# One kernel: adapter sums of the first network by single sequences, their rows spread through DRAM

## The reference

```
def lora_add(base, inp, A, B):
    Ab = A[layer_idx][lora_indices]      # per sequence: 16 x 512
    Bb = B[layer_idx][lora_indices]      # per sequence: 1376 x 16
    t = einsum('bri,bni->bnr', Ab, inp)
    return base + einsum('bor,bnr->bno', Bb, t) * SCALE     # SCALE = 0.5
gate = lora_add(einsum('bnh,fh->bnf', x, W_gate), x, A_gate, B_gate)
up   = lora_add(einsum('bnh,fh->bnf', x, W_up), x, A_up, B_up)
act  = silu(gate) * up
x    = x + ffn(lora_add(einsum('bnf,hf->bnh', act, W_down), act, A_down, B_down))
```

## Time and profile before

| | |
|---|---|
| median of 3 runs | 606.76 us (606.46 to 607.78) |
| the profiled execution | 606.15 us, span 604.5 us |
| PE busy in the span | 99% |
| DVE, ACT, POOL busy | 78%, 49%, 48% |

### The profile page before, as it was taken

The page is one execution under the profiler, slowest core; times in us unless marked ns, Lnnn a source line. Parts: engine busy times, 40 slices in busy tenths (PEclk is TensorE's granted clock), DMA queues, the critical chain, the costliest instruction groups (busy, mean ns, idle before and its releaser), DMA issues.

```text
span 604.5 us, 8075 instructions
## 1 busy us (share of the span) xinstructions
PE 599.7 (99%) x2904; PEld 491.9 (81%) x2904; DVE 469.7 (78%) x572; ACT 295.3 (49%) x413; POOL 292.7 (48%) x219
## 2 busy tenths in 40 slices
PE   8999999999999999999999999999999999999997
PEld 7787887878778888888888878888788888888886
DVE  6797757757778999873459877645879998999987
ACT  5865224323443445441124445334658886478860
POOL 6135334324434055831034586520005889958897
PEclk9999999999999999999999999999999999999999
DMA  8896472541171215212121200342232221322203
GB/s 255 220 227 180 148 170 65 131 130 28 53 207 37 71 35 166 69 31 66 35 71 35 70 30 31 84 83 84 61 101 78 77 69 36 109 67 75 75 7 139
DMA packets 30475, 56.06 MB, mean 93 GB/s; under 512 B 10468, under 2 KB 14532, under 8 KB 30052
## 3 DMA queue, kind: packets, MB, share of 16 engines
q1 hardware_dynamic: 28932, 53.05, 30.7%
q0 software_dynamic: 1216, 1.98, 1.5%
q10 hardware_dynamic: 288, 0.52, 0.2%
HBM read 48.44 MB, written 6.06 MB: 90 GB/s over the span
## 4 chain that ended last, share of the span: by engine, by line
PE 99%; DVE 0%; issue 0%
PE ps_down L2355 7%; PE ps_down L2356 7%; PE ps_down L2357 7%; PE ps_gate L2458 3%; PE ps_gate L2639 3%; PE ps_gate L2638 3%; PE ps_up L2638 3%; PE ps_gate L2459 3%; PE ps_gate L2460 3%; PE ps_up L2639 3%; PE ps_m L2638 3%; PE ps_down L2638 3%; PE ps_m L2639 3%; PE ps_down L2639 3%; PE ps_up L2458 3%; PE ps_up L2459 2%
## 5 line engine op out<-in xcount | busy, mean ns | idle before, releaser
L1144 POOL TENSOR_TENSOR up_sum<-up_sum,up_more 128x1024 f32<-128x1024 f32 x14 | 33.7, 2409 | 62.6 <-DVE up_more L1926 62.6
L2355 PE MATMUL ps_down<-act_hi,w_hi 128*128 128x512 f32 x112 | 43.9, 392 | 0.0
L2356 PE MATMUL ps_down<-act_lo,w_hi 128*128 128x512 f32 x112 | 43.6, 390 | 0.0
L2357 PE MATMUL ps_down<-act_hi,w_lo 128*128 128x512 f32 x112 | 43.6, 389 | 0.0
L1026 POOL TENSOR_TENSOR cond_total<-w_raw 128x512 f32<-128x512 f32 x8 | 10.5, 1310 | 60.4 <-DMA w_raw<-in_cond_gu 36.3
L1691 DVE TENSOR_TENSOR w_lo<-w_total,w_hi 128x512 fp32r<-128x512 f32 (+1 forms) x28 | 28.8, 1030 | 13.3 <-ACT w_hi L1462 12.6
L1926 DVE SCALAR_TENSOR_TENSOR gate_sum<-ps_up,s_group,gate_sum 128x1024 f32<-128x1024 f32 x28 | 35.8, 1279 | 3.8 <-PE ps_up L2639 3.7
L1102 POOL TENSOR_TENSOR act_lo<-up,act_hi 128x512 fp32r<-128x512 f32 x14 | 18.1, 1295 | 39.1 <-ACT act_hi L1468 39.1
L1156 POOL TENSOR_TENSOR act_lo<-gate_sum,act_hi 128x1024 fp32r<-128x1024 f32 x14 | 33.7, 2413 | 6.3 <-DVE gate_sum L1934 6.3
L1462 ACT ACTIVATE w_hi<-w_total 128x512 fp32r<-128x512 f32 (+1 forms) x28 | 20.7, 738 | 28.8 <-POOL w_total L1089 19.4
L1036 POOL TENSOR_TENSOR act_lo<-cond_out,act_hi 128x512 fp32r<-128x512 f32 (+1 forms) x14 | 19.1, 1389 | 28.9 <-ACT act_hi L1303 28.9
(11 more groups left out here) (413 smaller groups left out, 2031.5 us busy)
## 6 DMA issues: line engine op xcount, KB each, us to landing
w_int<-in_ffn_gu SPq DMA_DIRECT2D x14, 512.0 KB, 3.5
w_raw<-in_ffn_gu SPq DMA_DIRECT2D x10, 512.0 KB, 4.1
w_raw<-in_cond_gu SPq DMA_DIRECT2D x9, 512.0 KB, 5.9
w_raw<-in_ffn_dn SPq DMA_DIRECT2D x8, 448.0 KB, 3.2
w_int<-in_ffn_dn SPq DMA_DIRECT2D x8, 448.0 KB, 3.2
b_rows<-b_split SPq DMA_DIRECT2D x12, 256.0 KB, 4.6
xp<-in_x SPq DMA_DIRECT2D x8, 256.0 KB, 4.9
w_raw_third<-in_ffn_gu SPq DMA_DIRECT2D x4, 512.0 KB, 4.0
```

Source lines behind the costliest of these rows:

```text
L1144: nc.gpsimd.tensor_tensor(up_sum[:, u % 3, :], up_sum[:, u % 3, :], up_more[:, u % 2, :], ALU.add).then_inc(up_done, 1)
L2355: nc.tensor.matmul(ps[:, :], weights_hi[:, cols], rhs_hi(k), start=start and n == 0, stop=False)
L2356: nc.tensor.matmul(ps[:, :], weights_hi[:, cols], rhs_lo(k), start=False, stop=False)
L2357: last = nc.tensor.matmul(ps[:, :], weights_lo[:, cols], rhs_hi(k), start=False, stop=stop and n == len(ks) - 1)
```

## The change

`WARM` is 9. The start order is gate weights, first block of x, up weights, then the rest, and tile 0 of chunk 0 runs gate and up in turn per block of x. The adapter sums use `a_gu_raw` directly, one sequence (128 tokens) per matmul, with no ordering copies and no mask. ACT and DVE form one high and one low tile of 128x128 per chunk; SP stores the low ones and POOL the high ones to `t_split` in DRAM, and each then reads its half back into the blocks of `t_rows` that are not zero, in eight DMAs of 32 KB (16 partitions x 4 x 2 runs of 512 B in the two `g`). DVE zeroes `t_rows` once at the start. The weights of tile 1 are loaded ahead of `a_gu`. PE waits for both halves ahead of any adapter.

```diff
-WARM = 12
+WARM = 9
+        t_first_hi, t_first_lo = (place(f"t_first_{part}", [P, CH, P], F32R, at[home]) for part, home in (("hi", "t_hi"), ("lo", "gated")))
+        t_split = nc.dram_tensor("t_split", (2, NB, 2, R, P), F32, kind="Internal").ap()
-        start = [("w", 0)] + [("x", 0, k) for k in range(HK)] + [("w", 1)] + [("x", 1, k) for k in range(HK)]
+        start = [("w", 0), ("x", 0, 0), ("w", 1)] + [("x", 0, k) for k in range(1, HK)] + [("x", 1, k) for k in range(HK)]
+        def store_t(eng, half, c):
+            value = (t_first_hi, t_first_lo)[half][:, c, :]
+            eng.dma_start(t_split[half, c * BC:(c + 1) * BC].rearrange("s g r n -> (s g r) n"), value.bitcast(F32)).then_inc(t_stored[half], 16)
+        def spread_t(eng, half):
+            for q in (2 * half, 2 * half + 1):
+                for odd in range(2):
+                    rows = t_rows[q * PR + odd * R:q * PR + (odd + 1) * R, :, :].rearrange("r g (p e n) -> r g p e n", e=2, n=P)
+                    values = t_split[half].rearrange("(p e) g r n -> e g r p n", e=2)[odd]
+                    for g in range(2):
+                        eng.dma_start(rows[:, g, :, odd, :].bitcast(F32), values[g]).then_inc(t_copied[half], 16)
...
@@ SP
+            load(gu_a, 1)
             sp.wait_ge(ids_in[0], 16)
             indices = {b: sequence(sp, b) for b in range(BC, NB)}
             for b in range(BC, NB):
                 load_a_gu(sp, b, indices[b])
-            load(gu_a, 1)
...
             store_first(0)
-            copy_t(0)
+            for c in range(CH):
+                sp.wait_ge(t_first_lo_done, c + 1)
+                store_t(sp, 1, c)
             sp.wait_ge(b_stored[0], 16 * 2)
             spread_b(0)
-            copy_t(1)
+            sp.wait_ge(t_zero, 1)
+            sp.wait_ge(t_stored[1], 16 * CH)
+            spread_t(sp, 1)
             store_first(1)
@@ POOL, behind its a_dn loads
+            for c in range(CH):
+                pool.wait_ge(t_first_hi_done, c + 1)
+                store_t(pool, 0, c)
+            pool.wait_ge(t_zero, 1)
+            pool.wait_ge(t_stored[0], 16 * CH)
+            spread_t(pool, 0)
@@ ACT
-            for c in range(CH):
-                act.wait_ge(a_gu_in[c], 16 * BC)
-                for g in range(2):
-                    nc.scalar.activation(a_gu[...], ...).then_inc(a_gu_ready, 1)
...
             for n in range(2):
                 hi_of_b_first(n)
             cond_x_high(3)
             for c in range(CH):
-                hi_of_t(c, 2)
+                hi_of_first_t(c)
@@ DVE
+            nc.vector.memset(t_rows[:, :, :].bitcast(F32), 0.0).then_inc(t_zero, 1)
...
-            for n in (3, 1, 4):
-                cond_x_sum(n)
+            cond_x_sum(3)
             dve.wait_ge(w_hi_done, 1)
             lo(plain_lo[1][:, :], w_raw[:, 1, :], plain_hi[1][:, :]).then_inc(w_ready, 1)
             for n in range(2):
                 lo_of_b_first(n)
-            dve.wait_ge(mask_ready, 4)
+            cond_x_sum(1)
             for c in range(CH):
-                dve.wait_ge(t_sums, c + 1)
-                nc.vector.scalar_tensor_tensor(out=gated[:, c, 0:PT], in0=ps_m[:, pair_sums(c)], scalar=0.5, in1=seg_mask[:, :],
-                                               op0=ALU.mult, op1=ALU.mult).then_inc(t_masked, 1)
-                lo_of_t(c, 2)
+                lo_of_first_t(c)
+            cond_x_sum(4)
@@ PE
-                pe.wait_ge(t_copied[c], 16 * 2)
+                for half in range(2):
+                    pe.wait_ge(t_copied[half], 16 * 8)
...
+                if (t, c) == (0, 0):
+                    for k in range(HK):
+                        for g in range(2):
+                            last = part(g, range(k, k + 1))
...
+            def first_t():
+                for c in range(CH):
+                    pe.wait_ge(a_gu_in[c], 16 * BC)
+                    for k in range(HK):
+                        for q in range(4):
+                            sample = BC * c + q
+                            last = nc.tensor.matmul(ps_m[quarter(q), sample_sums(c)], a_gu_raw[:, sample, k * 2 * R:(k + 1) * 2 * R],
+                                                    xp[:, k, sample * P:(sample + 1) * P], start=k == 0, stop=k == HK - 1)
+                    last.then_inc(t_sums, 1)
...
                 plain_base(1, 0)
-                pe.wait_ge(t_masked, CH)
+                pe.wait_ge(t_first_lo_done, CH)
                 plain_base(1, 1)
```

More of the change, by code:

```diff
@@ L379, in adaln_ffn @@
         b_copied = [sem(f"b_copied{n}") for n in range(len(B_LOADS))]
-        t_copied = [sem(f"t_copied{c}") for c in range(CH)]
+        t_zero, t_first_hi_done, t_first_lo_done = sem("t_zero"), sem("t_first_hi_done"), sem("t_first_lo_done")
+        t_stored, t_copied = ([sem(f"{n}_{part}") for part in ("hi", "lo")] for n in ("t_stored", "t_copied"))
         a1_ready = sem("a1_ready")
@@ L1242, in hi_of_tail, with hi_of_first_t, hi_of_t @@
                 nc.scalar.activation(tail_hi[:, :, :], tail_raw[:, :, :], ACT.Copy).then_inc(tail_hi_done, 1)
[L1244 to L1253 removed]
+            def hi_of_first_t(c):
+                act.wait_ge(t_sums, c + 1)
+                nc.scalar.activation(t_first_hi[:, c, :], ps_m[:, sample_sums(c)], ACT.Copy, scale=0.5).then_inc(t_first_hi_done, 1)
+            def hi_of_t(c):
+                act.wait_ge(t_masked, c + 2)
+                nc.scalar.activation(t_hi[0:RB, c, 0:PT], gated[0:RB, c, 0:PT], ACT.Copy).then_inc(t_hi_done, 1)
+                for half in range(2):
+                    for row in (0, 1):
+                        last = nc.scalar.activation(t_rows[quarter(row), 0, pair_tokens(2 * c + half)], gated[quarter(half), c, 0:PT], ACT.Copy)
                 last.then_inc(t_hi_rows, 1)
             def hi_of_t_down():
[L1259 removed]
+                act.wait_ge(t_masked, 1)
                 nc.scalar.activation(t_hi[:, 0, 0:PT], gated[:, 0, 0:PT], ACT.Copy).then_inc(t_hi_done, 1)
@@ L1736, in lo_of_b_rest, with lo_of_first_t, lo_of_t @@
                 lo(b_lo[1][:, :], b_raw[1][:, :], b_hi_rest[:, :]).then_inc(b_ready, 1)
-            def lo_of_t(c, nets):
-                dve.wait_ge(t_hi_done, (0 if nets == 2 else CH + 1) + c + 1)
-                for g in range(nets):
-                    for half in range(2):
-                        rows = quarter(2 * g + half)
-                        for row in (2, 3) if nets == 1 else (2,):
-                            last = lo(t_rows[quarter(row), g, pair_tokens(2 * c + half)], gated[rows, c, 0:PT], t_hi[rows, c, 0:PT])
+            def lo_of_first_t(c):
+                dve.wait_ge(t_first_hi_done, c + 1)
+                nc.vector.scalar_tensor_tensor(out=t_first_lo[:, c, :], in0=ps_m[:, sample_sums(c)], scalar=0.5, in1=t_first_hi[:, c, :].bitcast(F32),
+                                               op0=ALU.mult, op1=ALU.subtract).then_inc(t_first_lo_done, 1)
+            def lo_of_t(c):
+                dve.wait_ge(t_hi_done, c + 2)
+                for half in range(2):
+                    rows = quarter(half)
+                    for row in (2, 3):
+                        last = lo(t_rows[quarter(row), 0, pair_tokens(2 * c + half)], gated[rows, c, 0:PT], t_hi[rows, c, 0:PT])
                 last.then_inc(t_lo_rows_done, 1)
             def lo_of_t_down():
-                dve.wait_ge(t_hi_done, CH + 1)
+                dve.wait_ge(t_hi_done, 1)
                 for c in range(CH):
@@ L2488, in plain_base, with part, input_ready @@
             def plain_base(t, c):
-                for g, ps in enumerate(plain_banks(t, c)):
-                    def input_ready(k, c=c, g=g):
+                def part(g, ks):
+                    def input_ready(k):
                         if t == 0:
                             pe.wait_ge(start_lo, max(started("w", g), started("x", c, k)))
-                    last = sums(ps, plain_hi[t], plain_lo[t], g * HK * P, range(HK), lambda k, c=c: h_hi[:, k, chunk(c)],
-                                lambda k, c=c: h_lo[:, k, chunk(c)], before=input_ready)
+                    return sums(plain_banks(t, c)[g], plain_hi[t], plain_lo[t], g * HK * P, ks, lambda k: h_hi[:, k, chunk(c)],
+                                lambda k: h_lo[:, k, chunk(c)], before=input_ready, start=ks.start == 0)
+                if (t, c) == (0, 0):
+                    for k in range(HK):
+                        for g in range(2):
+                            last = part(g, range(k, k + 1))
+                else:
+                    for g in range(2):
+                        last = part(g, range(HK))
                 if t == 0:
```

45 lines of the change are left out of this document (12 added, 33 removed).

## The result

| | before | after |
|---|---|---|
| median (range, runs) | 606.61 us (606.19 to 607.78, 6) | 609.95 us (609.34 to 610.56, 6) |
| profiled execution, span | 606.15, 604.5 | 610.54, 608.9 |
| mean granted clock of PE | 1.0 in the profiled execution | 0.994 in two of the six, 0.997 in four |

The change made the kernel slower: ratio 1.0053, 95% interval 1.0041 to 1.0066, +3.3 us. The forecast was 607.4, and the range ended at 609.3.

What follows compares the result with a forecast made beforehand. The prediction took PE's own sequence (99% of the chain) as the bound. PE, arriving at 31.1 us, would wait for rows until 33.6 instead of going on at 32.96: +0.65 us, 607.4 us in all, range 605.4 to 609.3.

Steps and rivals of the forecast that it cites:

- PE's start: Tile 0, chunk 0: PE starts about 1.0 us earlier, but the chunk ends at 12.6 against 12.82, -0.2 us.
- The bound of +1.3 us for a slow clock at the start: Tile 0: upper bound if the small gap holds PE's clock low for six matmuls more (6 x 0.2).
- The sums: Adapter sums on PE: 64 records take 2.0 us instead of 3.66, -1.7 us, bounds -1.8 and 0.
- Arrival, order and cover: PE reaches the first adapters at 31.1; zeroing `t_rows`, `a_gu_raw` and the tile 1 wait cost nothing.
- When the rows are there: Wait before the first adapters: rows land at 33.6, so PE waits 2.5 us and goes on +0.65 us later.
- 31.5 + 0.5 + 1.6 = 33.6: Rows' landing: `b_rows` at about 31.5, 0.5 for high rows alongside (0 to 1.1), 1.6 for low rows (1.1 to 2.0).
- Rival 2: Read-back: 16-partition writes are slower, last row at 34.6 or later; 608.4 to 609.5 us; chance 0.18.
- Rival 1: Read-back: the rows are earlier, PE goes on at 31.5 to 32.3; 605.3 to 606.1 us; chance 0.20.
- Rival 3: Behind the wait: PE's clock falls, 0.2 us per matmul for some 15 matmuls, +3 us, 610.4; chance 0.05.
- What is late next: Adapters of tile 2: `spread_b(1)` lands at about 42.2, just in time; PE's old sequence follows, moved by +0.65 us.
- Rival 4: First adapters: no wait at all, `b_rows` and rows by 31.1, the full 1.9 us gained; 604.9 us; chance 0.03.
- The sum: Whole kernel: profiled span 604.5 + 0.65 = 605.15, so 607.4 us on the scale of the median; chance 0.54.

Runs made afterwards that it cites:

- x2_start: Kernel before with only the new start (9 warm matmuls, new load order, gate and up in turn): 606.65 us, ratio 1.0004.
- x5_no_readback: Changed kernel without the 16 read-back DMAs of the rows, so the first net's adapters multiply zeros: 604.55 us, ratio 0.9964.
- x4_low_only: Changed kernel without POOL's eight read-backs of the high rows, PE waiting for the low rows only: 606.37 us, ratio 1.0001.
- y5: Changed kernel with each read-back DMA moving half its bytes, same count of DMAs and packets: 609.52 us, ratio 1.0046.
- y2: Changed kernel with each read-back DMA writing 32 partitions instead of 16, same DMAs, packets and bytes, rows misplaced: 608.59 us, ratio 1.004.
- y3: Changed kernel with read-back packets of 2 KB instead of 512 B, same DMAs and bytes, rows misplaced: 610.17 us, ratio 1.0043.
- z5: Changed kernel with t in a block layout, eight read-backs of 64 KB in place of sixteen of 32 KB: 609.24 us, ratio 1.0038.
- x1_fill: Changed kernel with 14 matmuls of zero weights in place of PE's idle time before the first adapters: 608.15 us, ratio 1.0031.
- z7_blocks_four: Changed kernel with block layout, 8 read-backs on three queues, all four quarters, four zero matmuls: 610.56 us, ratio 1.0069.
- z6_blocks_three: Changed kernel with block layout, 6 read-backs on three queues, product of low parts left out, two zero matmuls: 607.86 us, ratio 1.0021.
- z1_three_quarters: Changed kernel without the product of the two low parts: 12 read-backs on two queues, three `b_rows` DMAs: 609.29 us, ratio 1.0049.
- z3_queues_three: Changed kernel without the product of the two low parts, 12 read-backs shared by ACT, POOL and SP, four zero matmuls: 606.43 us, ratio 1.0001.
- x3_rows: Changed kernel with the old start (12 warm matmuls, old load order, gate then up): 610.18 us, ratio 1.0051.

## Why the prediction was wrong, step by step

**PE's start: nearly right in its result.** Chunk 0 of tile 0 ended at 12.92 (12.6 forecast, 12.82 before), 0.1 us later instead of 0.2 sooner, and `x2_start` shows 606.65 against 606.57. The path there was another: the first block of x landed at 5.88 by the trace, where before it was there at 4.50, so PE began at 7.32, after 1.45 us of idleness, and not at 5.9. I had taken that block to come as before. Chunk 0 ends near the old time nonetheless, as the clock rose sooner (6.35 us in the trace, 7.9 before).

```profile
3.55 0.63 ACT L1596 ACTIVATE plain_hi<-w_raw 128x512 fp32r<-128x512 f32 x1 [1.11 <-DMA w_raw<-in_cond_gu]
5.91 0.63 ACT L1600 ACTIVATE h_hi<-xp 128x512 fp32r<-128x512 f32 x1 [1.73 <-DMA xp<-in_x]
```

The bound of +1.3 us for a slow clock at the start was real all the same. In the profiled run of `x2_start` (607.93, its slowest), the matmuls behind the gap were still slow at 10.9:

```profile
7.32 0.80 PE L2355 MATMUL ps_down<-h_hi,plain_hi 128*128 128x512 f32 x1 [1.46 <-DVE h_lo L1691]
7.92 0.63 PE L2356 MATMUL ps_down<-h_lo,plain_hi 128*128 128x512 f32 x1
...
10.91 0.46 PE L2357 MATMUL ps_down<-h_hi,plain_lo 128*128 128x512 f32 x1
11.20 0.40 PE L2355 MATMUL ps_down<-h_hi,plain_hi 128*128 128x512 f32 x1
```

**The sums: right.** 64 records in 1.95 us (2.0 forecast): with half the columns they take half the time, so weight loads and issue didn't keep them near 3.6.

**Arrival, order and cover: right.** PE was through with tile 1 at 31.35 (31.1 forecast). Zeroing `t_rows` took 1.77 us, from 2.0 to 3.8, and delayed nobody. `a_gu_raw` was in time, and ahead of the second chunk of tile 1 PE didn't wait. The four `b_rows` DMAs were complete at 31.44 (31.5 forecast, before the half us for contention). That is partly luck: their issue began 0.8 us sooner than before (24.09 against 24.88), and they took 7.35 us from the first issue to the last landing, against 7.03 before and 6.88 in `x5_no_readback`.

**When the rows are there: the step that failed.** The forecast was "31.5 + 0.5 + 1.6 = 33.6"; measured 31.44 + 3.1 = 34.56. The last two terms, 2.1 us together, were 3.1. `x4_low_only` splits that: the low rows alone end 1.9 us behind `b_rows` (1.6 taken), and the high rows beside them add 1.2 (0.5 taken, for `b_rows` and the low rows together). The upper bounds, 2.0 and 1.1, do add up to 3.1, so what failed is the value taken and what it was priced by. I priced the low rows by the duration of other transfers of 256 KB, with a range for the partitions; but half the bytes (y5) and twice the partitions (y2) leave the tail as it is, and fewer DMAs shorten it (y3 against z5). The last copies of before moved those 256 KB in two DMAs; after has sixteen small ones in all. Rival 2 had the place right (34.6) and the cause, 16 partitions, wrong. Rival 1, rows at 31.5 to 32.3, fell.

By the Trainium skill, "DMA: Bandwidth & Descriptors", section "Anatomy of one DMA — SWDGE (gpsimd) path", 2.0 us plus bytes over 436 GB/s, an estimate for 32 KB is 2.1 us. The last ones took 5.4 us on SP and 5.7 on POOL, beside other transfers, so for this stretch the trace disagrees.

**What the wait does to PE: the chance was far too small.** Rival 3, "PE's clock falls in the wait", got 0.05 because no gap in before exceeded 0.4 us. It happened in all six runs. An absent row was read as evidence against it, where it was none. The sum thus held nothing for the clock. The size that the rival gave it, "some 15 matmuls: +3 us", was near (16 adapters and 6 full matmuls, 2.7 us in the profiled pair); over the medians it is 3.3 - 1.6 = 1.7 us, from `x1_fill`. Its time of 610.4 lies near the median in part by luck, since its rows came 1.0 us too early and its clock cost too much. The Trainium skill, "TensorE: Matmul & The Clock Gate", section "Why this matters for your kernels", warns that an idle gap between matmuls brings the clock down. The kernels with PE held agree, and show a chance rather than a certainty: one run in five with the gap of 1.35 us, two in four with that of 3.37.

**What is late next: right.** `spread_b(1)` ended at 42.88 (42.2 forecast), and PE, itself late, never waited for it. Rival 4 is `x5_no_readback`: 604.55 against the 604.9 worked out.

**The sum.** Forecast +0.65 us; measured +3.3. The missing 2.7 us are rows 1.0 us later than forecast (34.6 against 33.6) and 1.7 us of slow clock, which the sum had at nothing. Of the 3.3, about 1.6 us is the late rows at full clock: 34.65 - 32.96 = 1.7 in the trace and +1.6 in `x1_fill`. About 1.7 us is the clock. This isn't two independent losses: the wait is long because the sums got shorter, so PE comes 1.6 us sooner to rows that come 1.7 us later, and a gap of 3.2 us opens where there was none.

**Open.** Why one more small DMA landing behind `b_rows` goes with some 0.2 us isn't settled. One rival is untested: behind the rows SP issues `store_first(1)` and the weights of tile 3, 512 KB each, and these share the DMA engines while the last rows are awaited. In after, from 32.5 us until the last row landed, the profile shows only packets of SP's queue:

```profile
DMA packets 287, 0.61 MB, mean 298 GB/s; under 512 B 32, under 2 KB 32, under 8 KB 287
q1 hardware_dynamic: 287, 0.61, 108.9%
```

None of them has the 512 B of a row's piece: 32 are shorter and the others 2 KB or longer, so they belong to the transfers behind. By the profile the rows' packets had thus been sent by 32.5, while their landings came up to 34.56. No run moves those transfers away. Nor is it known why the profiled execution of `z7_blocks_four` has 2.9 us outside its span. `z6_blocks_three`, whose first adapter started 0.9 us earlier than in after, gained 2.1 of the 3.3 us and lost the clock in 6 of 12. That POOL's last high rows came at 35.81 in `z1_three_quarters` is a single trace. No version tried beats the kernel before; the best with rows is `z3_queues_three`, its equal, which leaves out the product of the two low parts.

## What to carry to other kernels

Time saved on the bounding engine ahead of a wait is worth nothing unless what it waits for comes sooner too; here it turned into idleness and then cost more, since the idleness brought the clock down. Where a copy is split into many small DMAs for the sake of layout, don't price it by its bytes alone: here the tail went with the number of DMAs that landed behind the transfer ahead of them. And if PE must wait a few us, price the slower matmuls behind the wait as well: a run with harmless matmuls in the gap tells how much that is.

## What the runs showed that I had not expected

- After a gap of 3.2 us PE ran at half clock for 5.8 us of nearly unbroken work (34.7 to 40.5 us); after one of 3.4 us, for over 3.3 us (36.5 to 39.8). By the traces the clock stays down for 6.8 us (after, 33.66 to 40.48; `z1_three_quarters`, 35.52 to 42.34) or for about 3.4 (y3, y5, z5). Whether a given gap brings it down differs between executions of one kernel: `x3_rows` fell in 5 of 7, `z5_blocks` in 8 of 10.
- The clock can fall after PE has gone on: 1.0 us after in `z5_blocks`, 0.9 in `y5_half_bytes`, 0.7 in `y3_long_rows`. The idle time ahead of it, 2.65 us in `z5_blocks`, had ended by then.
- The moment at which the clock first rises differs too: at 7.9 us in the profiled run of before, 6.35 in that of after, 11.0 in that of `x2_start`, though the last two have the same warm matmuls and the same gap of 1.45 us.
- A DMA of 32 KB into 16 partitions took 5.4 us to land at a DMA share of about 1, and in `y5_half_bytes` one of 16 KB took 5.0 us on SP (5.2 on POOL).
